# Reordering the per-head scan steps of a gated linear attention block, and moving a one-column copy from ScalarE to VectorE

## The reference, cut to what matters

```python
alpha = sigmoid((x @ Wg + bg) / 16)              # one decay per token and head
def step(state, inp):                            # state: 128 x 256 per head
    state = at[..., None, None] * state + kt[..., None] * vt[:, :, None, :]
    out_t = einsum('bhk,bhkv->bhv', qt, state)
out = (outs * sigmoid(x @ Wog)) @ Wo
x = x + layernorm(attn(layernorm(x)))
x = x + layernorm(ffn(layernorm(x)))
```

## Time and profile before

| | us |
|---|---|
| median of 2 runs | 7731.25 |
| lowest and highest | 7725.81 and 7736.69 |
| the profiled execution | 7734.95 |
| its span on the slowest core (core 5) | 7733.3 |
| spans of the 8 cores | 7679.8 to 7733.3 |

### The profile page before, as it was taken

How to read it: one execution, slowest core, us unless ns; L and a number is a source line. 1 busy time by engine, 2 the same in 40 slices (tenths; PEclk the granted TensorE clock), 3 DMA queues, 4 the chain that set the end, 5 groups by cost and what they waited for, 6 DMA issues and landing times.

```text
span 7733.3 us, 72123 instructions; the slowest of 8 cores (7679.8 to 7733.3 us)
## 1 busy us (share of the span) xinstructions
PE 4530.3 (59%) x21600; PEld 2082.7 (27%) x21600; DVE 2089.4 (27%) x4478; ACT 1575.7 (20%) x3527; POOL 246.9 (3%) x300
## 2 busy tenths in 40 slices
PE   3455544655544536455314777777777777778880
PEld 1122222222221222222101333333333333334440
DVE  2333333333222231322332222222222222221113
ACT  1222222122121121211231122222222222221112
POOL 0000000000100001000000000000000000000000
PEclk8666666666766757565556899999999999999995
DMA  2000000000512304022013111111121111111202
GB/s 56 11 11 15 19 11 11 11 22 1 66 20 32 31 20 44 6 38 22 21 33 47 22 22 22 22 22 22 22 38 29 22 22 22 22 22 22 44 1 84
DMA packets 265489, 200.21 MB, mean 26 GB/s; under 512 B 142020, under 2 KB 224068, under 8 KB 265110
## 3 DMA queue, kind: packets, MB, share of 16 engines
q0 software_dynamic: 244448, 128.23, 12.6%
q1 hardware_dynamic: 20662, 67.36, 2.5%
HBM read 307.00 MB, written 16.78 MB: 42 GB/s over the span
## 4 chain that ended last, share of the span: by engine, by line
PE 53%; ACT 16%; DVE 13%; issue 11%; DMA 5%; ACTq 1%; DVEq 1%; POOL 0%; POOLq 0%; SPq 0%
PE pb L158 53%; ACT h_sc L1072 4%; DVE S_state L575 2%; ACT cwb_sb L1054 2%; DVE st_s L359 2%; DVE st_sq L365 2%; DMA wog_buf<-Wog 2%; DVE khb L545 1%; ACT khT L561 1%; ACT xln_fm L406 1%; ACT expB L550 1%; DMA wq_buf<-Wq 1%; DMA wk_buf<-Wk 1%; ACT Sbf L781 1%; ACT xlnB L391 1%
## 5 line engine op out<-in xcount | busy, mean ns | idle before, releaser
L158 PE MATMUL pb<-x1ln_fm,w1g 128*128 128x384 bf16 (+1 forms) x7680 | 1341.7, 321 | 728.2 <-ACT h_sc L1072 408.5
L158 PE MATMUL pb<-w2g,h_sc 128*128 128x512 bf16 x5120 | 1192.1, 385 | 8.5 <-DVE h_sc L1079 8.5
L158 PEld LDWEIGHTS pb<-x1ln_fm,w1g 128*128 128x128 bf16 x7680 | 677.9, 101 | 1339.3 <-issue 1027.0
L1079 DVE TENSOR_TENSOR h_sc<-h_sc,cwb_sb 128x384 bf16<-128x384 bf16 (+1 forms) x768 | 258.1, 336 | 2025.5 <-ACT h_sc L1072 1984.5
L1072 ACT ACTIVATE h_sc<-pb,b1T_sb 128x384 bf16<-128x384 f32 (+1 forms) x768 | 419.9, 547 | 1320.5 <-PE pb L158 1320.4
L158 PEld LDWEIGHTS pb<-w2g,h_sc 128*128 128x128 bf16 x5120 | 504.1, 99 | 584.8 <-issue 42.4
L1113 DVE TENSOR_TENSOR acc<-acc,pb 128x512 f32<-128x512 f32 x640 | 439.9, 687 | 650.2 <-PE pb L158 595.0
L158 PE MATMUL pb<-Wv_sb,xln_fm 128*128 128x512 bf16 x2048 | 477.7, 399 | 0.0
L158 PE MATMUL pb<-v_tm,khT 128*128 128x256 bf16 x512 | 190.3, 372 | 398.0 <-ACT khT L561 316.5
L1054 ACT CAST cwb_sb<-pb 128x384 bf16<-128x384 f32 (+1 forms) x384 | 170.6, 444 | 964.0 <-PE pb L158 925.0
L575 DVE SCALAR_TENSOR_TENSOR S_state<-S_state,expB,pb 128x256 f32<-128x256 f32 x384 | 184.6, 481 | 538.1 <-PE pb L158 538.1
(11 more groups left out here) (145 smaller groups left out, 3767.1 us busy)
## 6 DMA issues: line engine op xcount, KB each, us to landing
w1g<-w POOLq DMA_DIRECT2D x64, 512.0 KB, 13.4
w2g<-w POOLq DMA_DIRECT2D x64, 512.0 KB, 15.0
x_tm<-x_pre SPq DMA_DIRECT2D x12, 2048.0 KB, 9.0
wog_buf<-Wog POOLq DMA_DIRECT2D x64, 256.0 KB, 4.6
x_tm<-x_own SPq DMA_DIRECT2D x4, 2048.0 KB, 7.7
wq_buf<-Wq POOLq DMA_DIRECT2D x32, 256.0 KB, 5.2
wk_buf<-Wk POOLq DMA_DIRECT2D x32, 256.0 KB, 5.2
x_sp<-x_tm SPq DMA_DIRECT2D x16, 512.0 KB, 2.6
```

Source lines behind the costliest of these rows:

```text
L158: fn = lambda E, o=out, l=lhsT, r=rhs, st=start, sp=stop: E.matmul(o, l, r, start=st, stop=sp)
L1079: b.op("v", lambda E, par=par, hc=hc, tscnt=tscnt: E.tensor_tensor(h_sc[:, par, hc, 0:tscnt], h_sc[:, par, hc, 0:tscnt], cwb_sb[:, par, 0: ...
```

## The change

1. `expB` becomes one tile of 8 columns, `expB_sb`, a column for each head, and the copy into it moves from ACT to DVE, right behind `khb`, in both scans.
2. In the prefix scan the loop emits `front(i)`, `back(i-2)`, `mid(i-1)` instead of `front`, `mid`, `back`.
3. ACT's copy `khT` also waits for the state update that was emitted last (`last_stt`).
4. The own scan is cut into parts, `s1` to `s6`, and these are emitted for different heads in one pass of the loop: all of head i up to `Sbf`, the output matmuls and the turn of head i-1, the v matmul and state update of head i-2, and `outog` and `khT` of head i-1. The kq matmul is emitted before `Dpre` instead of after it. A chunk is drained before `Wo`.

```diff
@@ prefix scan
-            b.wait("s", expB_rd[par])
-            b.wait("s", tkh)
-            tEB = pbread(b, bank6, "s", lambda E, par=par: E.copy(
-                expB_sb[par][:, :], bank6.sl(par * 256 + 127, 1)))
+            tEB = pbread(b, bank6, "v", lambda E, par=par, h=h: E.tensor_copy(
+                expB_sb[:, h:h + 1], bank6.sl(par * 256 + 127, 1)))
...
+            b.wait("s", last_stt[0])
             tkt = pbread(b, bank7, "s", lambda E, par=par: E.copy(
                 khT[par][:, :], bank7.sl(par * 128, 128)))
...
-        for i in range(n):
-            front(i)
-            if i >= 1:
+        for i in range(n + 2):
+            if i < n:
+                front(i)
+            if 2 <= i:
+                back(i - 2)
+            if 1 <= i <= n:
                 mid(i - 1)
-            if i >= 2:
-                back(i - 2)
@@ own scan
+                def s1(h):
...
+                    mm(b, bank4, bank4.sl(384, 128), isel8f[:, h * 128:(h + 1) * 128],
+                       bsc[:, c * C:(c + 1) * C], start=True, stop=True)
+                    mm(b, bank4, bank4.sl(0, 128), k_fm[:, h, c * C:(c + 1) * C],
+                       q_fm[:, h, c * C:(c + 1) * C], start=True, stop=True, seal=True)
...
+                for i in range(H + 2):
+                    if i < H:
+                        s1(i)
+                        s2(i)
+                    if 1 <= i <= H:
+                        s3(i - 1)
+                    if i >= 2:
+                        s5(i - 2)
+                        s6(i - 2)
+                    if 1 <= i <= H:
+                        s4(i - 1)
```

More of the change, by code:

```diff
@@ L274, in _build @@
     expB_rd = [None, None]
+    last_stt = [None]
     y_sb = sb("y_sb", [128, D], F32)
@@ L325, in _build @@
     Sbf = [msb(f"Sbf{p}", [128, DV], BF16) for p in range(2)]
-    expB_sb = [msb(f"expB{p}", [128, 1], F32) for p in range(2)]
+    expB_sb = msb("expB_sb", [128, H], F32)
     outog = msb("outog", [128, 16, 128], BF16)
@@ L538, in front @@
             par = i % 2
+            _ = h
             b.wait("t", tkR)
@@ L576, in back @@
                 S_state[:, h * DV:(h + 1) * DV], S_state[:, h * DV:(h + 1) * DV],
-                expB_sb[par][:, :], bank7.sl(256, 256), ALU.mult, ALU.add))
+                expB_sb[:, h:h + 1], bank7.sl(256, 256), ALU.mult, ALU.add))
             expB_rd[par] = tadd
+            last_stt[0] = tadd
         n = len(seq)
-        for i in range(n):
-            front(i)
-            if i >= 1:
-                mid(i - 1)
-            if i >= 2:
-                back(i - 2)
[L587 to L592, removed]
+        for i in range(n + 2):
[4 more added lines that the diff above has]
+            if 1 <= i <= n:
+                mid(i - 1)
     x_cons = [None]
@@ L736, in emit_own @@
                     b.wait(_e, tdo)
+            bank6, bank7 = pb[6], pb[7]
             for c in range(CCm):
                 ci = s * CCm + c
-                for h in range(H):
+                hst = {}
+                def s1(h):
                     par = h % 2
-                    bank6 = pb[6]
+                    bank4 = pb[4 + par]
                     b.wait("t", tkR)
@@ L750, in emit_own, with s2 @@
                        Rxm[:, c * C:(c + 1) * C], start=True, stop=True, seal=True)
+                    mm(b, bank4, bank4.sl(384, 128), isel8f[:, h * 128:(h + 1) * 128],
+                       bsc[:, c * C:(c + 1) * C], start=True, stop=True)
+                    mm(b, bank4, bank4.sl(0, 128), k_fm[:, h, c * C:(c + 1) * C],
+                       q_fm[:, h, c * C:(c + 1) * C], start=True, stop=True, seal=True)
+                def s2(h):
+                    par = h % 2
                     bank4 = pb[4 + par]
-                    mm(b, bank4, bank4.sl(384, 128), isel8f[:, h * 128:(h + 1) * 128],
-                       bsc[:, c * C:(c + 1) * C], start=True, stop=True, seal=True)
                     tdp = pbread(b, bank4, "v",
@@ L762, in emit_own @@
                     dpre_rd[par] = tdt
-                    mm(b, bank4, bank4.sl(0, 128), k_fm[:, h, c * C:(c + 1) * C],
-                       q_fm[:, h, c * C:(c + 1) * C], start=True, stop=True, seal=True)
                     b.wait("v", tdt)
@@ L767, in emit_own @@
                         smb[par][:, :], bank4.sl(0, 128), Dt[par][:, :], ALU.mult))
-                    tqt = pbread(b, bank6, "v", lambda E, bank6=bank6, par=par, c=c, h=h: E.tensor_tensor(
+                    tqt = pbread(b, bank6, "v", lambda E, par=par, c=c, h=h: E.tensor_tensor(
                         qtb[par][:, :], q_fm[:, h, c * C:(c + 1) * C],
                         bank6.sl(par * 256, 128), ALU.mult))
-                    tkh = pbread(b, bank6, "v", lambda E, bank6=bank6, par=par, c=c, h=h: E.tensor_tensor(
+                    b.wait("v", khb_rd[par])
+                    tkh = pbread(b, bank6, "v", lambda E, par=par, c=c, h=h: E.tensor_tensor(
                         khb[par][:, :], k_fm[:, h, c * C:(c + 1) * C],
                         bank6.sl(par * 256 + 128, 128), ALU.mult))
[L774 to L777, removed]
+                    tEB = pbread(b, bank6, "v", lambda E, par=par, h=h: E.tensor_copy(
+                        expB_sb[:, h:h + 1], bank6.sl(par * 256 + 127, 1)))
                     tprev = b.tok("v")
@@ L782, in emit_own, with s3 @@
                         Sbf[par][:, :], S_state[:, h * DV:(h + 1) * DV]))
+                    hst[h] = (tsm, tqt, tkh, tEB, tsb)
+                def s3(h):
+                    par = h % 2
+                    bank4 = pb[4 + par]
+                    tsm, tqt, tkh, tEB, tsb = hst[h]
                     b.wait("t", tsm)
@@ L794, in emit_own, with s5, s6, s4 @@
                        qtb[par][:, :], start=False, stop=True, seal=True)
+                    b.wait("t", tkh)
+                    mm(b, bank7, bank7.sl(par * 128, 128), khb[par][:, :],
+                       iI128b[:, :], start=True, stop=True, seal=True)
+                    khb_rd[par] = ("t", b.sem["t"][1])
+                def s5(h):
+                    par = h % 2
+                    b.wait("t", hst[h][5])
+                    mm(b, bank7, bank7.sl(256, 256), khT[par][:, :],
+                       v_tm[:, c, h * DV:(h + 1) * DV], start=True, stop=True, seal=True)
+                def s6(h):
+                    par = h % 2
+                    expB_rd[par] = pbread(
+                        b, bank7, "v", lambda E, par=par, h=h: E.scalar_tensor_tensor(
+                            S_state[:, h * DV:(h + 1) * DV],
+                            S_state[:, h * DV:(h + 1) * DV],
+                            expB_sb[:, h:h + 1], bank7.sl(256, 256),
+                            ALU.mult, ALU.add))
+                    last_stt[0] = expB_rd[par]
+                def s4(h):
+                    par = h % 2
+                    bank4 = pb[4 + par]
                     pbread(b, bank4, "v", lambda E, bank4=bank4, c=c, h=h: E.tensor_tensor(
@@ L800, in emit_own @@
                         og_fm[:, 2 * h + 1, c * C:(c + 1) * C], ALU.mult))
[L801 to L805, removed]
-                        khT[par][:, :], bank7.sl(par * 128, 128)))
[L807 to L813, removed]
+                    b.wait("s", last_stt[0])
+                    tkt = pbread(b, bank7, "s", lambda E, par=par: E.copy(
+                        khT[par][:, :], bank7.sl(par * 128, 128)))
+                    hst[h] = hst[h] + (tkt,)
+                for i in range(H + 2):
[9 more added lines that the diff above has]
+                        s4(i - 1)
                 tog_done = b.tok("v")
```

## The result

The changed kernel takes 7519.5 us (median of 11 runs), the kernel before 7711.6 (10 runs, those of the prediction among them). The ratio is 0.9748, 95% interval 0.9717 to 0.9778: faster by 2.5%. The forecast was 7525, 2.7% less. The profiled execution took 7550.3 us. In some executions of every kernel here the cores of one die run at a lower clock and take longer; the medians take in all runs, the ratios leave those out.

The account below looks back on a forecast made before the run. No single engine bounds the prefix scan, but a chain through three; the own scan is one head after another. Savings of 103 + 104 = 207 us from 7734.95 give 7528, set to 7525 for the median; range 7450 to 7640.

Parts of the forecast that it names:

- The sum: Whole kernel: 103 us saved in the prefix scans plus 104 in the own scan, 207 in all, giving 7525.
- The prefix ring: Prefix scan: chain of update, turn, khT, v matmul, update; falls from 2.28 to 2.00 us without the expB copy.
- the drain: End of the prefix scan before the change: state updates 2.00 us apart with no expB copy in the chain.
- the cover: Prefix scan: DVE finishes khb and copy 0.07 us before the v matmul's result; DVE's own ring 1.93.
- rival (d): Both scans: the copy makes DVE the bound; 7780 us at a copy price of 0.692; chance 0.04.
- The price of the copy: One-column expB copy on DVE, both scans: taken as 0.16 us, between bounds of 0.154 and 0.692.
- The own ring: Own scan, Dpre to Dpre: DVE's own row plus one trip to PE, 5.00 us against 5.77 before.
- The trip from the last `outog` to `Dpre`: Own scan, through PE's bsc and kq matmuls: 1.18 to 1.28 us, taken as 1.24; bounds 0.92 and 2.0.
- DVE's row: Own scan: DVE's work from Dpre to the end of the last outog, 3.76 us.
- (a): Prefix scan gains nothing because the ring over bank 7 is kept: 7627 us; chance 0.12.
- (b): Own scan gains little, outog putting the fp32 matmul on the ring: trip 1.9, ring 5.65, 7589 us; chance 0.14.
- (c): Both scans: denser PE work raises the clock from 0.50 to 2.4 GHz: 7435 us; chance 0.12.

Follow-up runs that it names:

- e1: Changed kernel with the prefix loop's old order (front, mid, back) restored, copy still on DVE: 7533 us, ratio 0.969 to the kernel before.
- e2: Changed kernel with the prefix scan's one-column copy back on ACT, new order kept: median 7634 us, ratio 0.968 to the kernel before.
- e3: Changed kernel with the prefix turn in banks 4 and 5 instead of 7, khT not waiting for the last update: 7224 us, ratio 0.932.
- e6: Changed kernel with the one-column copy made twice in the prefix scan: 7687 us (single time).
- e7: e1 (old prefix order, copy on DVE) with the one-column copy made twice in the prefix scan: 7570 us (single time).
- e9: Prefix v matmul and update in banks 7 and 6, against a kernel with turn, bsc/kq and Rx banks already split and copy on ACT: 7094 us, ratio 0.910.
- e5: Changed kernel with e3's prefix edits plus the own scan's bsc and kq matmuls in banks 2 and 3: 7182 us, ratio 0.928.

## Why the prediction was right, and where not

**The sum.** Forecast: 103 in the prefix and 104 in the own scan, 207 in all. Measured by scans: 86 and 102; by the medians, 7711.6 - 7519.5 = 192. Right in sign and in both places, with one term too large. That 7525 and 7519.5 lie so close is in part luck: I counted from 7731, the median of two runs, and the median of ten is 7711.6. From there the sum would have given 7505.

**The prefix ring.** That taking the copy from in front of `khT` gives 2.00, read off the drain, is right by e1 and e2. The step that failed is the cover: "Rx matmuls behind it 0.11 later (128 columns at 1.2 GHz), at 0.26; `khb` 0.54 after that, [...] at 0.80". The Rx matmul starts 0.20 after the turn (1819.52 to 1819.72) and `khb` 0.57 after it, so `khb` starts at 0.91 from the end of an update, not at 0.80, and DVE's ring is 2.05 instead of 1.93. I had called this the tightest place with 0.07 to spare; it was 0.05 short. By what I had written down myself this part is wrong: the update was to wait for the v matmul and the ring to close at 2.00, and DVE without idle time before the update was the sign of rival (d). The 31 intervals of a scan are 63.9 us on average where I had 62.9, which over 12 scans makes 12 of the 17 us between 103 and 86. Most of the rest is that I took the last scan for all: its 31 intervals before are 70.2 us, the mean of the twelve is 69.8. What misled me was taking the distance of two matmuls from their columns and not from a row: the turn has a weight tile of 128 rows and the Rx matmul one of 8, and where a matmul follows one of the other kind the rows show some 0.1 more (last section). What is left is `khb`, 0.57 behind the Rx matmul and not 0.54.

**The price of the copy.** I took 0.16; the row after is 159 ns:

```profile
L550 DVE COPY expB_sb<-pb 128x1 f32<-128x1 f32 x384 | 61.0, 159 | 40.4 <-DVE khb L547 1.3
```

The pair of small reductions had said 5 ns more for PSUM than for SBUF, and it was 159 against 154. The Trainium skill, "Perfetto Trace Analysis", section "Optimizing Scalar/DVE Operations", would have made it some 65 ns dearer, about 0.22, an estimate from its figures. The trace does not agree: the row is 159 ns long, and the update starts 0.26 after the copy's start, with the same 0.10 between them that stands between `khb` and the copy.

**The own ring.** Forecast 5.00, measured 4.99, but two terms were off and cancelled. The trip from the last `outog` to `Dpre` is 1.30, not 1.24: 0.15 to PE as said, then 1.15 from `bsc` to `Dpre`, that is 0.92 and 0.23 for the kq matmul in between, where I had 0.11 for it and some of 0.10 for the weights. It may be the same term as in the prefix ring, since `bsc` has 8 rows and kq 128; but here the type changes too, from fp32 to bf16, and the rows do not part the two. DVE's row is 3.69, not 3.76, since `smb` now follows `Dpre` by 0.98 and not by 1.05. The kq matmul, which came behind `Dpre` before (2171.77), is now done ahead of it, so that only ACT's `Dt` is waited for; that this is the reason is argued and not tried. That the two errors cancel to 0.01 is luck. Chunk: 39.5 forecast, 39.6 to 40.1 measured.

**The rivals.** (a), no gain in the prefix because the ring over bank 7 is kept: the ring was kept, as e3 shows (1.24 with the turn in banks of its own), but the gain came, since the copy was inside the ring. (b), a dearer trip: 1.30, not 1.9. (c), the clock: both scans stayed at 0.50. (d), DVE as the bound: this is what the prefix scan is now, by e6 and e7, but at a copy of 0.16 and so only by 0.05; its price of 0.692 was far off.

**Half and half.** What I did not see is that the two edits of the prefix loop do the same thing. With either the interval is 2.00 (e1, e2), with both 2.05 (changed kernel). The second is not only unneeded but costs about 2 us in each scan.

## What to carry to other kernels

When an instruction leaves a queue in which it delayed another, draw the ring of the engine that takes it as carefully as the one that is relieved, with start-to-start distances from rows and not from sizes; a cover of under 0.1 us out of 2 is no cover. Ask of each wait in a ring if it is the data's or a buffer's: here both scans turned on a PSUM bank shared by two uses, and giving these a bank each (in the prefix with one wait of ACT dropped) brought 300 us and about 105 us, against the 190 of the whole reordering. After each ring is opened, read the rows again before naming the next one: the third change of banks (e9) brought nothing.

## What I had not expected of the hardware

The distance from one matmul's start to the next was longer in these rows where the two had different numbers of rows. At a clock of 0.50 the four output matmuls, all of 128 rows and 128 columns, follow each other by 0.10 to 0.11, and so does the v matmul the turn, in the own scan of the changed kernel:

```profile
2067.42 0.31 PE L158 MATMUL pb<-qtb,Sbf 128*128 128x128 bf16 x1
2067.53 0.31 PE L158 MATMUL pb<-smb,v_tm 128*128 128x128 bf16 x1
2067.64 0.31 PE L158 MATMUL pb<-qtb,Sbf 128*128 128x128 bf16 x1
...
2067.74 0.31 PE L158 MATMUL pb<-iI128b,khb 128*128 128x128 bf16 x1
2067.85 0.42 PE L158 MATMUL pb<-v_tm,khT 128*128 128x256 bf16 x1
```

But from the turn (128 rows) to the Rx matmul (8 rows) it is 0.20, and from an Rx matmul to a v matmul, in e5, 0.24:

```profile
1530.30 0.31 PE L158 MATMUL pb<-Rxm,isel8b 8*128 8x128 bf16 x1
1530.54 0.39 PE L158 MATMUL pb<-v_tm,khT 128*128 128x256 bf16 x1
1530.72 0.31 PE L158 MATMUL pb<-iI128b,khb 128*128 128x128 bf16 x1
```

In the prefix of the changed kernel the Rx matmul follows the turn by 0.20 in all 348 pairs that have no wait between them. In the experts, at a clock of 1.00, a matmul of 64 rows (`selg`) follows one of 128 rows and 512 columns (`w2g`) by 0.31 in 205 pairs, where two of 128 rows and 512 columns are 0.22 apart. That the change of rows is the cause is what these rows suggest; no run took it alone.
